# A linear-attention kernel whose tiles run their sixteen 256-column matmuls in one row

## The reference

```python
k = heads(key, Wk, bk, Sk)            # context of 12544 tokens x 512
v = heads(value, Wv, bv, Sk)
k_prime = relu(einsum('bhnd,fd->bhnf', k, Wkf)) * attention_mask
kv = einsum('bhnf,bhne->bhfe', k_prime, v)
k_sum = sum(k_prime, axis=2)
```

## Time and profile before

| what | us |
|---|---|
| median of three executions | 855.77 (855.35 to 855.78) |
| the profiled execution's own time | 855.42 |
| its span, first to last instruction | 853.6 |
| PE busy | 847.2 (99%) |
| DVE, ACT, POOL busy | 679.7, 563.8, 376.3 |

### The profile page before, as it was taken

The page is one execution under the profiler, slowest core; times in us unless marked ns, Lnnn a source line. Parts: engine busy times, 40 slices in busy tenths (PEclk is TensorE's granted clock), DMA queues, the critical chain, the costliest instruction groups (busy, mean ns, idle before and its releaser), DMA issues.

```text
span 853.6 us, 14403 instructions
## 1 busy us (share of the span) xinstructions
PE 847.2 (99%) x4608; PEld 730.2 (86%) x4608; DVE 679.7 (80%) x1059; ACT 563.8 (66%) x1025; POOL 376.3 (44%) x221
## 2 busy tenths in 40 slices
PE   9999999999999999999999999999999999999998
PEld 7888888888888888888888888888888889878887
DVE  5877777777777777777777777888888878879997
ACT  6666666666666666666666666666777756677695
POOL 2655554445455554454455544454555533220210
DMA  7312123010101010010101010010101000489850
GB/s 274 99 50 97 53 75 146 27 47 25 49 25 49 25 47 26 25 49 25 49 25 49 25 42 31 25 49 25 49 25 50 26 1 1 178 315 410 320 185 13
DMA packets 19530, 66.26 MB, mean 78 GB/s; under 512 B 2224, under 2 KB 2992, under 8 KB 19120
## 3 DMA queue, kind: packets, MB, share of 16 engines
q1 hardware_dynamic: 19072, 64.88, 21.5%
q10 hardware_dynamic: 432, 1.05, 0.3%
HBM read 65.66 MB, written 0.26 MB: 77 GB/s over the span
## 4 chain that ended last, share of the span: by engine, by line
PE 98%; DVE 1%; DMA 0%; ACT 0%; issue 0%; DVEq 0%; ACTq 0%
PE side_ps L816 21%; PE side_ps L817 21%; PE side_ps L818 20%; PE kv_ps L929 11%; PE side_ps L916 11%; PE kv_ps L1213 4%; PE side_ps L1026 2%; PE side_ps L1032 2%; PE side_ps L1036 1%; PE side_ps L824 1%; PE kv_ps L824 1%; PE side_ps L1007 1%; PE kv_ps L1075 1%; DMA early<-in_wk 0%; PE kv_ps L1032 0%; PE kv_ps L1036 0%
## 5 line engine op out<-in xcount | busy, mean ns | idle before, releaser
L463 POOL TENSOR_TENSOR ksum_acc<-ksum_acc,kf 128x1024 f32<-128x1024 f32 x97 | 233.1, 2403 | 85.2 <-DVE kf L1316 85.2
L456 POOL TENSOR_TENSOR ctx_lo<-ctx_raw,ctx_hi 128x512 fp32r<-128x512 f32 x92 | 120.5, 1310 | 273.3 <-ACT ctx_hi L553 273.3
L561 ACT ACTIVATE keys<-side_ps,bias_cols 64x512 fp32r<-64x512 f32 (+1 forms) x196 | 132.5, 676 | 148.0 <-PE side_ps L818 143.0
L1292 DVE SCALAR_TENSOR_TENSOR keys<-side_ps,bias_cols,keys 64x512 fp32r<-64x512 f32 (+1 forms) x196 | 144.8, 739 | 83.8 <-ACT keys L561 80.5
L1309 DVE TENSOR_TENSOR kf<-side_ps,fb 128x256 f32<-128x256 f32 x392 | 148.7, 420 | 15.6 <-ACT fb L578 4.3
L816 PE MATMUL side_ps<-wv_hi,ctx_lo 128*128 128x512 f32 x392 | 153.9, 393 | 0.0
L817 PE MATMUL side_ps<-wv_lo,ctx_hi 128*128 128x512 f32 x392 | 153.7, 392 | 0.0
L818 PE MATMUL side_ps<-wv_hi,ctx_hi 128*128 128x512 f32 x392 | 152.5, 389 | 0.0
L816 PE MATMUL side_ps<-ctx_hi,wk_lo 128*128 128x512 f32 (+1 forms) x384 | 148.9, 388 | 0.0
L817 PE MATMUL side_ps<-ctx_lo,wk_hi 128*128 128x512 f32 (+1 forms) x384 | 148.8, 388 | 0.0
L818 PE MATMUL side_ps<-ctx_hi,wk_hi 128*128 128x512 f32 (+1 forms) x384 | 147.7, 385 | 0.0
(11 more groups left out here) (209 smaller groups left out, 967.7 us busy)
## 6 DMA issues: line engine op xcount, KB each, us to landing
ctx_raw<-in_ctx SPq DMA_DIRECT2D x46, 512.0 KB, 3.3
early<-in_stream SPq DMA_DIRECT2D x15, 1024.0 KB, 8.1
raw<-in_stream SPq DMA_DIRECT2D x12, 1024.0 KB, 9.3
early<-in_stream SPq DMA_DIRECT2D x8, 512.0 KB, 4.6
early<-in_ctx SPq DMA_DIRECT2D x2, 512.0 KB, 6.9
early<-in_wv SPq DMA_DIRECT2D x1, 1024.0 KB, 7.6
early<-in_wq SPq DMA_DIRECT2D x1, 1024.0 KB, 9.1
early<-in_wo SPq DMA_DIRECT2D x1, 1024.0 KB, 5.2
```

What stands on the lines that cost most here:

```text
L456: pool.tensor_tensor(ctx_lo[:, s, :, cols], raw[:, :, t % 2 * P:(t % 2 + 1) * P], ctx_hi[:, s, :, cols].bitcast(f32), ALU.subtract).then_i ...
L463: pool.tensor_tensor(ksum_acc[:, :].rearrange("p (j f) -> p j f", f=P), ksum_acc[:, :].rearrange("p (j f) -> p j f", f=P), kf[:, t % 2, :, ...
L561: act.activation(keys_2[rows, s, 2 * m + h, 0:n], src[rows, 0:n], ACT.Identity, bias=bias_cols[rows, KC + m:KC + m + 1]).then_inc(k_hi_rea ...
L1292: dve.scalar_tensor_tensor(out=keys_2[other, s, 2 * m + h, 0:n], in0=src[rows, 0:n], scalar=bias_cols[rows, KC + m:KC + m + 1], in1=keys_2 ...
```

## The change

The 66 tiles 4 to 69 (periods 1 to 16 and the first two tiles of period 17) get an order of their own; the tiles before and after keep the old one.

- **PE** (`period_burst`): jobs 0 and 1, `key_values` of the tile before, jobs 2 and 3, then twelve keys matmuls, then the values of the next tile. Jobs and keys share three banks that take turns with `t` (`burst_banks`): job 1's bank is also where the keys go.
- **ACT** (`tile_burst`): for job 1 it copies both halves out of the bank (one more 256-column copy), so that DVE can make this sum later from SBUF alone. The high part of the features is copied in two halves of 512 columns, within the tile itself instead of in the next one. The context split comes last.
- **DVE** (`tile_burst`): sums in the order 0, 2, 1, 3, with `values_low` after the first; mask and low part in two halves of 512 columns.
- **POOL** (`period_burst`): waits for `kf_lo_ready`, adds the features, and splits the context tile after that. Before, it split first, and added when the mask was done.
- The row sums and twelve small weight splits for the later layers move to tiles 70 to 90 (they stood in tiles 68 to 87).

```diff
+BURST, BURST_TILES = LAST - 7, 2
+        def burst_banks(t):
+            return [f_ps[0], k_bank, f_ps[1], f_ps[0]] if t % 2 else [f_ps[0], f_ps[1], k_bank, f_ps[0]]
 # GpSimd
+            def period_burst(c, s, tiles=TILES):
+                n = TILES * c
+                for t in range(tiles):
+                    pool.wait_ge(kf_lo_ready, n + t + 1)
+                    add_features(n + t, t)
+                    split_ctx_low(n + 2 * TILES + t, s, t)
 # ScalarE
+            def burst_share(n, t, i, slot):
+                act.wait_ge(f_done, JOBS * n + i + 1)
+                act.wait_ge(fsum_ready, JOBS * n + (0, 0, 1, 2)[i])
+                both = burst_banks(t)[i].rearrange("p (j x f) -> p j x f", j=2, x=2)
+                last = act.activation(fb[:, slot, :, :], both[:, :, 1, :], ACT.Copy)
+                if i == 1:
+                    act.wait_ge(ksum_added, n - 1)
+                    act.wait_ge(kf_lo_ready, n - 1)
+                    last = act.activation(kf[:, t % 2, 2:4, :], both[:, :, 0, :], ACT.Copy)
+                last.then_inc(fb_ready, 1)
+            def tile_burst(n, t, keys, split):
+                burst_share(n, t, 0, 0)
+                burst_share(n, t, 1, 1)
+                values_high(n, t, False)
+                burst_share(n, t, 2, 0)
+                burst_share(n, t, 3, 0)
+                act.wait_ge(kf_left_ready, n - TILES + 1)
+                act.activation(kf_2[:, t % 2, 0:4, 0, :], kf[:, t % 2, 0:4, :], ACT.Copy).then_inc(kf_left_hi_ready, 1)
+                act.wait_ge(kf_ready, n + 1)
+                act.activation(kf_2[:, t % 2, 4:8, 0, :], kf[:, t % 2, 4:8, :], ACT.Copy).then_inc(kf_hi_ready, 1)
+                keys_high(*keys)
+                split_ctx_high(*split)
 # TensorE
+            def burst_job(c, s, n, t, i):
...
+                if i == 0:
+                    pe.wait_ge(fsum_ready, JOBS * n)
+                if i == 2:
+                    pe.wait_ge(k_lo_ready, 2 * (KC * (c + 1) + t))
+                if i == 3:
+                    pe.wait_ge(fsum_ready, JOBS * n + 1)
...
+            def burst_keys(c, s, n, m):
+                pe.wait_ge(ctx_lo_ready, TILES * c)
+                pe.wait_ge(fb_ready, JOBS * n + 2)
...
+            def period_burst(c, s, tiles=TILES):
+                n = TILES * c
+                for t in range(tiles):
+                    for i in (0, 1):
+                        burst_job(c, s, n + t, t, i)
+                    key_values(n + t - 1, t + 1)
+                    for i in (2, 3):
+                        burst_job(c, s, n + t, t, i)
+                    burst_keys(c + 1, 1 - s, n + t, t)
+                    if t == TILES - 1:
+                        values(n + t + 1, 1 - s, 0, ())
+                    elif t < tiles - 1:
+                        values(n + t + 1, s, t + 1, ())
...
-            with pe.Fori(1, LAST - 3, 2) as c:
+            values(TILES, 1, 0, ())
+            with pe.Fori(1, BURST, 2) as c:
+                period_burst(c, 1)
+                period_burst(c + 1, 0)
+            period_burst(BURST, 1, BURST_TILES)
+            period(BURST, 1, start=BURST_TILES)
 # VectorE
+            def tile_burst(n, t, keys):
+                left, right = slice(0, NPAIR // 2), slice(NPAIR // 2, NPAIR)
+                burst_sum(n, t, 0, 0)
+                values_low(n, t)
+                burst_sum(n, t, 2, 0)
+                burst_sum(n, t, 1, 1)
+                burst_masked(n, t, left, 3, kf_left_ready)
+                burst_sum(n, t, 3, 0)
+                burst_masked(n, t, right, 4, kf_ready)
+                burst_low(t, left, kf_left_hi_ready, n - TILES + 1)
+                burst_low(t, right, kf_hi_ready, n + 1).then_inc(kf_lo_ready, 1)
+                keys_low(*keys)
```

More of the change, by code:

```diff
@@ L590, in features_high_half, with tile @@
                 act.activation(kf_2[:, t, js, 0, :], kf[:, t, js, :], ACT.Copy).then_inc(kf_hi_ready, 1)
-            def tile(n, t, first=False, keys=(), splits=()):
+            def burst_share(n, t, i, slot):
[20 more added lines that the diff above has]
+                split_ctx_high(*split)
+            def tile(n, t, first=False, keys=(), splits=(), former=True):
                 for i in range(2):
                     features_share(n, i, first and t == 0)
-                if not (first and t == 0):
+                if former and not (first and t == 0):
                     features_high(n - 1, t - 1)
@@ L674, in _ @@
                 tile(t, t, first=t < 2, keys=((1, 1, t, k_bank, CHUNK),), splits=((4 + t // 2, 0, t),))
[L675 to L682, removed]
+            features_high(TILES - 1, TILES - 1)
+            with act.Fori(1, BURST, 2) as c:
+                period_burst(c, 1)
+                period_burst(c + 1, 0)
+            period_burst(BURST, 1, BURST_TILES)
+            period(BURST, 1, start=BURST_TILES, former=False)
+            for c in range(BURST + 1, LAST - 2):
+                period(c, c % 2)
             period(LAST - 2, 0, splits=LAST_TILES)
@@ L1336, in masked_features_last, with burst_sum, burst_masked, burst_low @@
                    .then_inc(kf_ready, 1)
-            def tile(n, t, first=False, keys=()):
+            def burst_sum(n, t, i, slot):
+                if i == 0:
+                    dve.wait_ge(ksum_added, n - 1)
+                    dve.wait_ge(kf_lo_ready, n - 1)
+                dve.wait_ge(fb_ready, JOBS * n + i + 1)
+                sums = kf[:, t % 2, 2 * i:2 * i + 2, :]
+                high = burst_banks(t)[i].rearrange("p (j x f) -> p j x f", j=2, x=2)[:, :, 0, :]
+                dve.tensor_tensor(sums, sums if i == 1 else high, fb[:, slot, :, :], ALU.add).then_inc(fsum_ready, 1)
+            def burst_masked(n, t, js, sums, ready):
+                dve.wait_ge(fsum_ready, JOBS * n + sums)
+                dve.tensor_scalar(kf[:, t % 2, js, :], kf[:, t % 2, js, :], 0.0, mask[:, bass.ds(n, 1)], ALU.max,
+                                  ALU.mult).then_inc(ready, 1)
+            def burst_low(t, js, high, count):
+                dve.wait_ge(high, count)
+                return dve.tensor_tensor(kf_2[:, t % 2, js, 1, :], kf[:, t % 2, js, :],
+                                         kf_2[:, t % 2, js, 0, :].bitcast(f32), ALU.subtract)
+            def tile_burst(n, t, keys):
[10 more added lines that the diff above has]
+                keys_low(*keys)
+            def tile(n, t, first=False, keys=(), former=True):
                 features_sum(n, t, 0, first)
@@ L1343, in tile @@
                     queries_out()
-                else:
+                elif former:
                     features_low(n - 1, t - 1)
@@ L1389, in row_sum, with period_burst, period @@
                    .then_inc(row_sums_ready, 1)
-            def period(c, s, keys=CHUNK, pieces=0, sums=None):
+            def period_burst(c, s, tiles=TILES):
                 n = TILES * c
[L1393 to L1399, removed]
+                for t in range(tiles):
+                    tile_burst(n + t, t, (c + 1, 1 - s, t, burst_banks(t)[1], CHUNK))
+            def period(c, s, keys=CHUNK, start=0, former=True):
+                n = TILES * c
+                for t in range(start, TILES):
+                    i = sum_behind(n + t)
+                    if i == 0:
+                        dve.wait_ge(sums_loaded, 16 * 2)
+                    if 0 <= i < 2 * KC:
+                        row_sum(i // KC, i % KC)
+                    i = piece_behind(n + t) - 1
+                    if 0 <= i < 3 * KC:
+                        qkv_low(i)
+                    tile(n + t, t, keys=((c + 1, 1 - s, t, k_bank, keys),), former=former or t > start)
             def queries_out():
@@ L1448, in _ @@
                 tile(t, t, first=t < 2, keys=((1, 1, t, k_bank, CHUNK),))
[L1449 to L1460, removed]
+            features_low(TILES - 1, TILES - 1)
+            with dve.Fori(1, BURST, 2) as c:
+                period_burst(c, 1)
+                period_burst(c + 1, 0)
+            period_burst(BURST, 1, BURST_TILES)
+            period(BURST, 1, start=BURST_TILES, former=False)
+            for c in range(BURST + 1, LAST):
+                period(c, c % 2, keys=HALF if c == LAST - 1 else CHUNK)
             tile_before_last(NT - 2, 0)
```

64 lines of the change are left out of this document (48 added, 16 removed).

## The result

| | before | changed |
|---|---|---|
| median, us (6 executions each) | 855.56 (855.35 to 855.78) | 870.95 (869.11 to 871.20) |
| profiled execution, own time | 855.42 | 869.11 |
| span | 853.6 | 867.3 |

The ratio is 1.0173 (95% interval 1.0163 to 1.0183): 1.7% slower. The profiled execution is one of two at a granted clock of 1.000 over the whole span (869.1 and 869.6 us); the other four have 0.998 and take 870.9 to 871.2.

What follows compares the result with a forecast made beforehand. PE, busy 847.2 us and 98% of the chain, was taken as the bound. 855.42 - 1.3 (merged runs) + 15.2 (stalls) = 869.3, or 869.7 us for the median; range 862 to 882, to hold 8 in 10.

Steps and rivals of the forecast that it cites:

- The stall at the keys, once a period: PE's keys at the first tile of periods 2 to 17 wait for POOL's context split: 16 x 0.95 = +15.2 us.
- rival A: The forecast itself: PE stalls at the keys once a period, median 869.7 us; chance 0.79.
- the masks: On DVE, left mask laid out at 3.38 to 3.87 and right at 4.44 to 4.93, each waiting 0.12 us.
- The merged runs: On PE, one run of 512-column matmuls in place of two saves 0.02 us a tile, -1.3 us over 66 tiles.
- rival D: On PE, the run of sixteen is torn by a wait for sum 0: 877 us; chance 0.04.
- The added wait on POOL: POOL's add waits for kf_lo_ready at about 6.3, so its split ends 2.71 us into the next tile; +15.2 us.
- The add beside PSUM operations: POOL's add now runs beside DVE's keys_low and sum 0, which read PSUM: worth 0.
- SP's loads: The half's load, issued after POOL's split, lands at 6.2 and ACT wants it at 7.05: hidden by 0.85 us.
- the moves at the ends: Values of tile 4 first, tile 3's features' high part at once, old order from tile 70: within 0.3 us, 0 taken.
- The row sums: Row sums and weight splits move two or three tiles later, under PE in the old order as before: 0.
- Rival B: No stall at PE's keys, the chain to kf_lo_ready 0.95 us shorter than laid out: 854.4 us; chance 0.09.
- Rival C: ACT and DVE become the bound, their loop having 0.23 us to spare: 889 to 901 us; chance 0.08.

Runs made afterwards that it cites:

- e3_ctx_between: Changed kernel with ACT's context high part between the feature halves and POOL splitting before adding, still behind kf_lo_ready: 855.04 us, ratio 0.9995 to the kernel before.
- e7_both: Changed kernel with ACT's context part between the feature halves, POOL splitting first, and tile 70's context part behind the keys: 854.94 us, ratio 0.9993 to the kernel before.
- e1_split_first: Changed kernel with POOL splitting the context tile before waiting for kf_lo_ready and adding, ACT's order kept: 901.36 us, ratio 1.0535 to the kernel before.
- e2_no_lo_wait: Changed kernel with POOL's wait for kf_lo_ready removed, add still ahead of split: 910.96 us, ratio 1.0648 to the kernel before.

## Why the prediction was right, and where it was off

- **The stall at the keys, once a period** (rival A): right in place, cause and count, 16. The term was 0.95 us each and is 0.78, so 12.4 us in place of 15.2. The step that was mis-sized is the masks: I gave each 0.12 us of waiting and no overlap with the next instruction, since the earlier trace rows show it for one. In the trace the left mask did wait (0.13), but sum 3 starts 0.09 before that mask ends, and the right mask starts 0.03 after sum 3. With it `kf_lo_ready` came at 6.11 and not 6.31. The split ended 2.47 us into the next tile in place of 2.71, and the first matmul behind the stall, 0.1 longer than its kind, gave part of that back. Everything before that lies on the layout to 0.02 us (sum 0 at 0.85, values_low 1.90, left mask 3.38). The bounds on this term were narrower than their own wording: counted out on the layout, overlaps of 0.08 everywhere and masks that do not wait bring `kf_lo_ready` 0.51 earlier and not 0.35, and no overlap on ACT or DVE at all some 0.46 later. The result lies well inside either.
- **The merged runs:** tiles of 7.38 as the fixed part of a run has it, and no tear in the run of sixteen (rival D). The gain of 0.02 a tile is in every tile, and 0.6 us of the 1.3 is given back at tile 70. The rule of the Trainium skill that the prediction cites ("TensorE: Matmul & The Clock Gate"), by which the order would be worth nothing, has the trace against it here.
- **The added wait on POOL** was priced as a cost alone. The prediction did not ask what the wait guards: without it the kernel is 55 us slower than before, not 15.4. Its trace of the kernel before held the sign of it. The low part that the add reached into took 1.45 us, and the prediction set that against two halves of 0.68; the right measure is the same instruction's own mean, 1.24 us (page of the kernel before, part 5):

```profile
L1322 DVE TENSOR_TENSOR kf<-kf 128x1024 fp32r<-128x1024 f32 x96 | 119.2, 1242 | 12.2 <-ACT kf L584 12.2
```

- **The add beside PSUM operations**, priced at 0, was right: `keys_low` takes 1.53 us beside the add (325.65, the add at 325.70). It was no news either, for in the kernel before it takes 1.53 (304.03) with the add (303.23 to 305.63) beside it.
- **SP's loads, "hidden by 0.85 us", and the moves at the ends, "within 0.3 us":** the first holds in the 66 tiles. The second is the step that failed. I laid out ACT's need for the load in the new order only. In tile 70 the old order asks for the same load 4.5 us before it has landed (555.80 against 560.34), and it cost 2.3 us, with some 1.6 more in the executions at 0.998. The row sums, moved to the same tile and priced at 0, stand ahead of sums for which PE waits there, 0.45 us in the changed kernel. That 869.7 came so near to 870.95 is partly luck, errors that cancel: 2.8 too much for the stalls, 2.8 and the clock too little at the end.
- **Rival B** (no stall) needed what `e3_ctx_between` and `e7_both` then made by another order, and its price, 854.4, is near their 855.0 and 854.9. What is missing is the 0.63 us at tile 70.
- **Rival C** (ACT and DVE the bound) did not occur in the change. The margin of 0.23 us was too small: ACT's context part ends at 326.83, and ACT stands idle for 0.5 us until PE's next job (327.33), or 0.6 with the overlap of 0.10 that the layout allows. In the layout ACT was 0.36 later. `e1_split_first` shows that the margin is finite: 1.2 us more on one instruction made every tile 0.7 longer.

## What to carry to other kernels

When a wait is put ahead of an instruction on an engine that "has nothing to do", lay out what is queued behind it and for whom: here POOL was 43% busy and still on the path once a period. Put first what is waited for (here the split, not the add), then choose the time of the rest by what it would exclude. Where an order changes from one schedule to another, lay out the first tile of the second with the loads of the first: a load that is early enough in both can be late between them, and work that was moved to that tile can stand in front of what it waits for.

## What the runs showed of the hardware

- A VectorE addition with both inputs in SBUF took 1.59 us instead of 0.41 under a GpSimd add (`e1_split_first`), and the half low parts 1.70 on average instead of 0.69 (`e2_no_lo_wait`); operations with one input in PSUM took the same as alone (0.69 and 0.42). GpSimd's own add took 2.78 for 2.41 where it started 0.16 us after a low part (`e2_no_lo_wait`).
- A run of 512-column matmuls behind 256-column ones costs some 0.03 us once: after twelve and after four of them by the earlier trace rows, and with one such change less in a tile of the new order, whose run has sixteen, tiles of 7.38 in place of 7.40.
- Behind one gap of 2.1 us on PE, matmuls ran at the lower clock from about 320.3 to 323.7 us in two profiles of the kernel with 34 tiles; its executions at 0.998 took 1.2 to 1.7 us longer than the one at 1.000. Behind gaps of 0.8 us every 30 us the clock stayed at 1.00. In three profiles with the same long gap it stayed there too.
